# Causal attention and feed network: query tiles outermost, the feed's steps between the score blocks

## The reference

```
x = x + layernorm(attention(layernorm(x)))    # causal, low-rank terms added to every weight
h = layernorm(x)
for blk in range(3):
    h = h + linear2(gelu(layernorm(linear1(h)) * gamma + beta))    # 256 to 256, 4-bit weights scaled
x = x + layernorm(h)
```

## Time and profile before

| | us |
|---|---|
| median of 3 runs (1530.27 to 1532.49) | 1530.82 |
| the profiled execution, its own time | 1532.92 |
| its span in the trace | 1531.2 |
| of it: weights and projections, to the first score product | 177.3 |
| attention, to the last product with v | 1031.1 |
| feed | 322.8 |

### The profile page before, as it was taken

How to read it: one execution, slowest core, us unless ns; L and a number is a source line. 1 busy time by engine, 2 the same in 40 slices (tenths; PEclk the granted TensorE clock), 3 DMA queues, 4 the chain that set the end, 5 groups by cost and what they waited for, 6 DMA issues and landing times. The chain is left out here.

```text
span 1531.2 us, 27338 instructions
## 1 busy us (share of the span) xinstructions
PE 1415.8 (92%) x8838; PEld 621.7 (41%) x8838; DVE 319.3 (21%) x871; ACT 1218.0 (80%) x1552; POOL 315.9 (21%) x938
## 2 busy tenths in 40 slices
PE   6899499999989999998999998999999879997995
PEld 2455222222322223232223232222232558886784
DVE  3366100000000000000000000000000285578756
ACT  1366399999979999997999998999999555545644
POOL 0121100000120000021000012000010166446754
PEclk7699699999989999998999999999999999998998
DMA  5165751001130110022001012100000310011001
GB/s 142 60 227 190 140 128 28 29 29 28 49 93 1 28 28 29 29 71 71 24 6 29 29 45 79 45 2 1 1 1 8 129 58 1 1 56 55 1 1 55
DMA packets 60327, 77.62 MB, mean 51 GB/s; under 512 B 16016, under 2 KB 31376, under 8 KB 60176
## 3 DMA queue, kind: packets, MB, share of 16 engines
q1 hardware_dynamic: 52704, 68.79, 15.4%
q10 hardware_dynamic: 7472, 6.92, 1.8%
HBM read 50.50 MB, written 25.17 MB: 49 GB/s over the span
## 5 line engine op out<-in xcount | busy, mean ns | idle before, releaser
L729 ACT ACTIVATE probs<-S 128x1024 f32<-128x1024 f32 (+3 forms) x1152 | 981.3, 1173 | 70.8 <-PE S L761 67.0
L779 PE MATMUL O<-probs,vg 128*32 128x512 f32 (+3 forms) x4608 | 578.8, 575 | 0.6 <-POOL probs L702 0.5
L761 PE MATMUL S<-q_op,k_op 64*128 64x512 f32 (+3 forms) x2304 | 502.4, 480 | 44.4 <-DMA k_op<-qk_rows 17.4
L761 PEld LDWEIGHTS S<-q_op,k_op 64*128 64x128 f32 x2304 | 213.7, 187 | 604.8 <-ACT probs L729 562.3
L702 POOL TENSOR_SCALAR_AFFINE_SELECT probs<-probs 128x256 f32<-128x256 f32 x256 | 102.7, 406 | 928.1 <-ACT probs L729 919.7
L929 PE MATMUL psC<-wfT,yTC 128*128 128x256 f32 x768 | 175.1, 386 | 7.9 <-ACT yTC L990 5.5
L741 DVE COPY acc<-O 128x512 f32 x16 | 11.1, 691 | 777.1 <-PE O L779 777.1
L929 PEld LDWEIGHTS psC<-wfT,yTC 128*128 128x128 f32 x768 | 146.6, 194 | 29.5 <-ACT yTC L990 7.1
L779 PEld LDWEIGHTS O<-probs,vg 128*32 128x32 f32 x4608 | 91.5, 108 | 138.6 <-issue 118.3
L977 ACT ACTIVATE yC<-uC,nmrC,rstdC 128x256 f32<-128x256 f32 x128 | 66.3, 590 | 56.4 <-POOL nmrC L93 56.3
L984 ACT COPY yTC<-psC 128x1024 f32<-128x1024 f32 x32 | 31.6, 1007 | 56.0 <-PE psC L922 56.0
(11 more groups left out here) (96 smaller groups left out, 729.7 us busy)
## 6 DMA issues: line engine op xcount, KB each, us to landing
qk_rows<-parts SPq DMA_DIRECT2D x32, 512.0 KB, 3.1
q_op<-qk_rows SPq DMA_DIRECT2D x256, 64.0 KB, 2.3
k_op<-qk_rows SPq DMA_DIRECT2D x240, 64.0 KB, 2.3
acc_sums<-acc SPq DMA_DIRECT2D x16, 256.0 KB, 2.1
xC<-in_L_attn_x SPq DMA_DIRECT2D x8, 512.0 KB, 4.8
acc<-acc_sums SPq DMA_DIRECT2D x4, 1024.0 KB, 6.3
out<-uC SPq DMA_DIRECT2D x8, 512.0 KB, 3.1
acc<-in_L_attn_x ACTq DMA_DIRECT2D x6, 512.0 KB, 4.7
```

The costliest lines, as they stand in the source:

```text
L729: nc.scalar.activation(probs[:, pair % NP, :, 0:TT - q0], S[:, pair % NS, :, 0:TT - q0], ACT.Exp, scale=SCALE).then_inc(exp_ok, 1)
L761: last = nc.tensor.matmul(S[:, pair % NS, a, 0:TT - q0], k_op[mine, pair % 2, kb * P:(kb + 1) * P], q_op[mine, pair % 2, j * TT + q0:(j + ...
L779: last = nc.tensor.matmul(O[h * STRIP:(h + 1) * STRIP, o % 2, q0:TT], vg[:, kb, h, :], probs[:, (2 * b + h // 2) % NP, h % 2, 0:TT - q0], ...
```

## The change

The stages `attend` and `feed` become one, `attend_and_feed`, and the loops of the attention are turned inside out. Query tiles come first, in rising order, then the 4 groups, which makes 32 visits (`VISITS`); a visit goes through the key blocks of its tile from the diagonal down. As soon as a tile's four visits are done its feed can begin, in two halves of 256 tokens. A planner, `plan()`, places the 22 PE steps of a tile's feed between the blocks of later visits: from block 26 on, one tile per 76 blocks, and onto the end of a visit where one is within 1.7 blocks. Of the 154 steps of tiles 0 to 6, 27 stand at the end of a visit. The last tile's 22 steps follow the last block. It also fixes the order of the work on DVE, ACT, POOL and SP by a simulated run with costs that are written into it (full exponential 0.14 + 0.735, product 1.8, turn 0.6, layernorm 3.3, gelu 3.6, eight-DMA load 3.6).

`q_op` and `k_op` are now rings: 3 slots of a tile for q, 8 slots for k, so that each of the 144 chunks of keys (one tile of keys for one visit) is loaded anew. `O` has one buffer, and one PSUM bank `F` serves the feed. DVE turns `O` in 32 by 32 squares (`turn_o`), divides, turns back, and SP moves the result with 4 DMAs to `attT`. Layernorm including the inverse square root is on DVE alone. The gelu stands among the exponentials on ACT. V is kept as 17 columns per head for all heads, so the copies from `v_all` to `vg` on POOL go away. PE waits once per block for both pairs.

```diff
-                    for pair in (2 * b, 2 * b + 1):
-
-                        pe.wait_ge(exp_ok, i * NPAIR + pair + 1)
...
+                    if first and v:
+                        pe.wait_ge(o_out, v)
...
+                def score(b):
+                    v, t, c, kb, q0 = BLOCKS[b]
+                    if b == 0 or BLOCKS[b - 1][0] != v:
+                        pe.wait_ge(q_in[v % QS], LOAD * (v // QS + 1))
+                    if kb % NB == 0:
+                        pe.wait_ge(k_in[c % RING], LOAD * (c // RING + 1))
+                    if 2 * b + 1 >= NS:
+                        pe.wait_ge(exp_ok, 2 * b + 2 - NS)
+                    for n in (2 * b, 2 * b + 1):
+                        for a in range(2):
...
+    steps = {}
+    boundary = [LAST[v] + LAG for v in LAST]
+    for t in range(NT - 1):
+        for n, (name, k) in enumerate((name, k) for name in STEPS for k in range(2)):
+            at = FEED_FROM + FEED_EACH * (t + n / (2 * len(STEPS)))
+            near = min(boundary, key=lambda b: abs(b - at))
+            at = near if abs(near - at) < 1.7 else int(at)
+            steps.setdefault(at, []).append((name, t, k))
+    pe = []
+    for b in range(NBLK + LAG):
+        if b < NBLK:
+            pe.append(("score", b))
+        if b >= LAG:
+            pe.append(("weigh", b - LAG))
+        pe += steps.get(b, [])
+    pe += [(name, NT - 1, k) for name in STEPS for k in range(2)]
...
+                    else:
+                        m, t = int(x[0][-1]), x[1]
+                        for k in range(2):
+                            act.wait_ge(dve_ok[k], done[f"copy{m}", t, k])
+                        for c in range(NC):
+                            col = m * NC + c
+                            last = nc.scalar.activation(zT[:, c, :], zT[:, c, :], ACT.Gelu, bias=g["beta"][:, col:col + 1],
+                                                        scale=g["gamma"][:, col:col + 1])
+                        last.then_inc(gelu_ok, 1)
...
+                    if x[0] == "turn_o":
+                        v = x[1]
+                        dve.wait_ge(pv_ok, LAST[v] + 1)
+                        if v:
+                            dve.wait_ge(o_ready, v)
+                        nc.vector.transpose(o_turned[:, :, :].rearrange("p b e -> p (b e)"), O[:, :]).then_inc(o_out, 1)
+                        continue
...
+                for x in order["SP"]:
+                    if x[0] == "k_load":
+                        c = x[1]
+                        v, s = CHUNKS[c]
+                        if c >= RING:
+                            sp.wait_ge(scored, 2 * CHUNK_END[c - RING] + 2)
+                        with sp.Fori(0, 1):
+                            load_rows(sp, d, k_op[:, c % RING, :, :], 1, VISITS[v][1], slice(s * TT, (s + 1) * TT), k_in[c % RING], LOW + need)
...
+                    for b in range(NB):
+                        last_v = nc.vector.tensor_tensor(v_heads[:, bass.ds(n * NB + b, 1), :, 0:D].rearrange("p o h e -> p (o h) e"),
+                                                         psV[:, b, :].rearrange("p (h e) -> p h e", e=D),
+                                                         g["bv"][:, :].rearrange("p (h e) -> p h e", e=D), ALU.add)
```

More of the change, by code:

```diff
@@ L612, in _ @@
                         pe.sem_inc(op_used, 1)
-def attend(nc, g, d):
+HT = TT // 2
+HB = HT // P
+LAG = 2
+NS, NP = 3, 6
+RING, QS, AS = 8, 3, 3
+VISITS = [(t, i) for t in range(NT) for i in range(NG)]
+CHUNKS = [(v, s) for v, (t, i) in enumerate(VISITS) for s in range(t, -1, -1)]
+BLOCKS = [(v, t, c, s * NB + b, b * P if s == t else 0)
+          for c, (v, s) in enumerate(CHUNKS) for t in (VISITS[v][0],) for b in range(NB)]
+NBLK = len(BLOCKS)
+LAST = {v: n for n, (v, _, _, _, _) in enumerate(BLOCKS)}
@@ new lines, with feed_parts @@
+CHUNK_END = {c: n for n, (_, _, c, _, _) in enumerate(BLOCKS)}
+DIAG = [n for n, (_, t, _, kb, _) in enumerate(BLOCKS) if kb >= t * NB]
+STEPS = ["project", "turn_x"] + [f"{x}{m}" for m in range(BLK) for x in ("first", "turn", "second")]
+FEED_FROM, FEED_EACH = 26.0, 76.0
+def feed_parts():
+    parts = [("x_load", "SP", 1.0, ()), ("project", "PE", 1.8, ("moved",)), ("evac_att", "DVE", 0.75, ("project",)),
+             ("ln_att", "DVE", 3.3, ("evac_att",)), ("add_x", "DVE", 1.2, ("ln_att", "x_load")), ("ln_x", "DVE", 3.3, ("add_x",)),
+             ("norm_x", "DVE", 0.5, ("ln_x",)), ("turn_x", "PE", 0.6, ("norm_x",)), ("copy_x", "DVE", 0.75, ("turn_x",))]
+    h_at = "copy_x"
+    for m in range(BLK):
+        out = f"add{m}" if m < BLK - 1 else "evac_h"
+        parts += [(f"first{m}", "PE", 1.8, (h_at,)), (f"evac{m}", "DVE", 0.75, (f"first{m}",)), (f"ln{m}", "DVE", 3.3, (f"evac{m}",)),
+                  (f"norm{m}", "DVE", 0.5, (f"ln{m}",)), (f"turn{m}", "PE", 0.6, (f"norm{m}",)),
+                  (f"copy{m}", "DVE", 0.75, (f"turn{m}",)), (f"second{m}", "PE", 1.8, (f"gelu{m}",)),
+                  (out, "DVE", 0.8, (f"second{m}",))]
+        h_at = out
+    return parts + [("ln_h", "DVE", 3.3, ("evac_h",)), ("result", "DVE", 1.1, ("ln_h",)), ("store", "SP", 0.5, ("result",))]
@@ new lines, in attend_and_feed @@
+def attend_and_feed(nc, g, d):
+    order, _ = plan()
+    done = {}
+    for e in ("PE", "DVE"):
+        total = [0, 0]
+        for x in order[e]:
+            if len(x) == 3:
+                total[x[2]] += 1
+                done[x] = total[x[2]]
+    steps = [x for x in order["PE"] if len(x) == 3]
+    place = {x: n for n, x in enumerate(steps)}
+    gelus = {x: n + 1 for n, x in enumerate(x for x in order["ACT"] if x[0] != "exp")}
+    cuts = {n: m + 1 for m, n in enumerate(x[1] for x in order["POOL"])}
@@ L631, in attend @@
[L631 to L655, removed]
+        two = lambda n, s: [sb(f"{n}{k}", s)[(slice(None),) * len(s)] for k in range(2)]
+        vg = g["vg"]
+        k_op = sb("k_op", [P, RING, PAIRS, TT], F32R)
```

697 lines of the change are left out of this document (326 added, 371 removed).

## The result

| | before | after |
|---|---|---|
| median of 4 runs each on one chip, us | 1531.65 (1530.27 to 1533.18) | 1677.82 (1675.55 to 1678.74) |
| ratio, 95% interval | | 1.0952 (1.0933 to 1.0971) |
| span of the profiled execution | 1531.2 | 1675.7 |

The change makes the kernel 9.5% slower. The forecast was 1496 us, range 1445 to 1562, with 0.27 on slower. It had the wrong sign, and the time lies outside the range.

What follows compares the result with a forecast made beforehand. ACT paced the old attention; PE was to become the bound between the blocks. Block 48 at 272, plus 1097 to 1369, 33 for the last full blocks to 1402, tail 92: 1494, with 1.7 outside 1496 us, range 1445 to 1562.

Steps and rivals of the forecast that it cites:

- rival 2: Visit ends: the turn of O waits behind DVE's layernorm or a later step, 2.6 us more each, +62, 1558; chance 14%.
- Rival 3: Full blocks: four score products take PE itself 0.83 us, not 0.66, so no room exists, +70, 1566; chance 6%.
- rival 4: Better hiding: visit ends filled fully, half the stalls gone, the clock holds in the tail, 1448; chance 20%.
- rival 1: Longer table switches: each gelu stops ACT for 2.4 us more than taken, +50, 1546; chance 8%.
- the stall of a gelu: Between the blocks: PE stalls 2.6 us at each of 21 gelus while ACT is away, 55 us.
- the single wait: PE's one wait per block for both pairs was taken to be worth 0 by itself.
- The feed's steps: Feed products and turns between blocks 48 and 557: 198 us of PE work, plus 15 for weight loads laid bare.
- The start: Up to block 48, paced by SP's loads, then the second tile's last visit and three feed steps: block 48 at 272.
- The tail: Last tile's bare feed after the last block, thrice 16.7 us in it: 92 us, 5 for the clock, bounds 83 and 105.
- The middle: Block 48 to the last product with v, 1130 us: PE work 1018, gelu stalls 55, visit ends 24, last full blocks 33.
- the visits' ends: PE waits at each visit's end for DVE's turn of the single O: 1.0 us net per end, 24 us.
- room in the full blocks: PE needs 1.66 us of a full block's 1.833, so 0.17 us to spare per block for feed steps.

Runs made afterwards that it cites:

- e4: The kernel after without the feed of tiles 0 to 6 (attention and the last tile's feed stay): 1348.40 us, ratio 0.8804 to the kernel before.
- e2: The kernel after with each feed product of tiles 0 to 6 cut into two halves one block apart: 1690.48 us, ratio 1.1038.
- e11: e10 with the feed's steps placed from block 30 on, 77 blocks per tile, instead of 26 and 76: 1533.10 us, ratio 1.0002.
- e5: The kernel before with a single wait per block for both pairs and nothing else: 1535.56 us, ratio 1.0021.
- e3: The kernel after with PE again waiting for each pair's slot alone: 1647.77 us, ratio 1.0759.
- e1: The kernel after with the feed's gelu replaced by an exponential, so the table loads go and the feed's values change: 1583.75 us, ratio 1.0341.
- e9: The kernel after with the first three loads of queries issued by ACT instead of SP: 1670.45 us, ratio 1.0901.
- e12: e10 with the feed's steps placed from block 34 on, 75 blocks per tile: 1542.90 us, ratio 1.0065.
- e8: The kernel after with the second half of the last tile's feed steps writing to a free score bank: 1669.20 us, ratio 1.0893.
- e10: The kernel after with the edits of e3, e7, e8 and e9 together, the last tile keeping the gelu: 1540.49 us, ratio 1.0065.
- e7: The kernel after with the gelu computed from a polynomial on DVE and a tanh on ACT: 1591.07 us, ratio 1.0383.

## Why the forecast was wrong

**Right.** The front (0), the first score product (180.18 for 180.3), the skeleton's attention (e4: from block 48 on 941 us, where 949 go by the old pace), the length of a gelu on ACT (4.13 for 4.3; the 0.3 for lost overlap isn't there), key loads hidden after tile 2 (PE has no wait for one there), and PE as the bound between the blocks (e2, e11). Its 7.5 us from step to step takes every step for a product; by its own 29.5 us per tile it is 7.1, still above ACT's 6.3. DVE is 36% busy in the middle (457.7 of 1269), less than the 45% given, and PE's waits for the turn of `O` come to some 7 us in the whole run, so rival 2 is out. The two rows count the same waits, once for the load of the weights and once for the products behind it:

```profile
PEld O L929 <- DVE o_turned L1028: 6.7, 4, 5.6
PE O L929 <- DVE o_turned L1028: 5.8, 2, 5.4
```

Rival 3 fell with e5, rival 4 with the result itself, and rival 1 had the right place with the wrong price: the switch is no longer than I took, what it does to PE is.

**The step that failed: the stall of a gelu, "(4.3 + 0.97 - 2.65) = 2.6 x 21 = 55".** It is mis-sized in each of its last two terms (0.97 stands there for the 0.92 of the sentence before it, which makes 1 us and isn't what failed). For 2.65 us of work left to PE the timeline shows one block, 1.86 from 887.40 to its end at 889.26. For one exponential to be waited for, it shows two, 1.99: that is the single wait, and e3 has one. 4.13 + 1.99 - 1.86 gives the stop of 4.26. Even the gelu without table loads stops PE, for 1.45 us on average in e1, where my formula gave nothing; 21 of those are 30 us. And the clock behind the stop was no term at all, though the earlier trace rows had shown me 0.68 on a PE that is idle for most of a stretch; I had put it into the tail alone. The table loads' part of this, stop and clock, is 94 us by e1. With the 30 that stay in e1 the gelus cost some 124 us where the forecast had 55.

**"The single wait by itself is worth 0."** It costs some 3 us in the kernel before and 30 in the new one. The argument ("where PE bounds, neither wait holds") looked at blocks in steady stream only, and left out the block behind each feed step.

**The feed's steps.** I took 1.83 us for a product with its exposed load and 0.54 for a turn. The timeline of the kernel after has:

```profile
858.03 1.99 PE L969 MATMUL F<-zT,wfT 128*128 128x256 f32 x8
859.96 0.73 PE L913 MATMUL S<-q_op,k_op 64*128 64x512 f32 x4
...
879.54 0.66 PE L960 MATMUL F<-ident,yC 128*128 128x128 f32 x4
880.13 0.73 PE L913 MATMUL S<-q_op,k_op 64*128 64x512 f32 x4
```

That is 1.93 and 0.59 from start to start: 98 x 0.10 + 56 x 0.05 = 13 us. That is too little to change the sign.

**The start, +25.7.** In e4, without the feed, block 48 starts at 285.3. The forecast without its 2.7 us for feed steps is 269.3, so 16 us are lost without any feed: a load takes SP 3.8 to 4.0 us, as reckoned, but a move 2.4 instead of 1.9, and the visits wait for queries that stand behind moves. By e9 SP's queue has a part in it; how the 16 divide no run shows. The first feed steps take 12.4 us (297.7 - 285.3) where I had 2.7, another 9.7. The timelines of SP and PE in the kernel after:

```profile
272.66 2.43 SPq L857 DMA_DIRECT2D attT<-o_div  x4
275.20 3.88 SPq L489 DMA_DIRECT2D q_op<-qk_rows  x8
```

```profile
264.36 1.09 PE L960 MATMUL F<-ident,yC 128*128 128x128 f32 x4 [7.92 <-DVE yC L1018]
```

PE reached the turn 7.9 us before its layernorm was done, DVE being in the layernorms of both halves. That is close to the wait that I had named as the one that would make the forecast wrong, though PE waits here for what the turn reads and not for the bank. It isn't the main cause: e12 has it with 8.1 us and e11 with 3.7.

**The tail, +29.8.** The first part came out: 6.3 us to the first product, as predicted, and 18.8 from there to the first turn for 19.8. In the whole tail six products take 3.4 to 3.8 us instead of 1.99 and five turns 1.09 instead of 0.63, 12.5 us where I had 5 for the clock; the bank costs 8.6 by e8. What is left, 29.8 - 7.5 - 8.6 or about 14 us, no run took apart. The place is known: the forecast has "thrice 16.7", and from the first product of a block to the next block's it is 30.3 us (1585.5 to 1615.8) and 24.1 (to 1639.9). In the first of them DVE takes 13.1 us from the first evacuation to the last copy, where I had 9.5.

**The middle, +126.** The tanh and the wait per pair take 120 us out of it (1256 to 1136 in e10), where the forecast had 55 for all stalls of gelus. The other 61, which e10 still has over the forecast without those 55, are what follows.

**Why there was no gain even without the stops.** e11's middle takes 1134 us, close to the 1130 of the forecast by chance, since those contained 55 of gelu stalls. Without them the forecast is 1075. Of the 59 us between, 13 are the dearer steps. The other 46, with the 24 reckoned for the visits' ends, make 70 us; the window of e11 has PE idle for 1134.0 - 1085.8 = 48 of them, and its clock of 0.98 makes some 20 more as an estimate (2% of 1086). What PE waited for in e11's middle can be read off (columns as in the earlier trace rows):

```profile
PE F L980 <- DVE yC L1044: 23.8, 8, 6.4
PE S L931 <- ACT probs L904: 18.0, 24, 1.8
```

Half of the 48 are eight waits of the feed's turns for their layernorm on DVE, the longest 6.4 us; 18 are waits for exponentials. The forecast had nothing for the first kind in the middle. Whether another order on DVE would avoid them stays open.

The balance against the kernel before can be written out with e11. The start takes 25 us more than at the old pace (284 for 259). The middle at the old pace would be 949, so it takes 185 more: 213 + 13 of feed steps, less 72 of room in the full blocks (414 x 0.173) and 40 on the diagonals (24 x 1.66), plus the 70. The tail is 113. That is 25 + 185 + 113 = 323 us for the feed, and the stage that was dissolved took 322.8. This must come out so, since e11 takes as long as the kernel before and the 70 were found as the rest; it sorts the costs and proves none. The room of 72 and 40 us is the forecast's, which no run measures by itself. Measured are the start, the tail, PE's 48 idle us and its clock, and they, with the dearer steps, are what eats the gain. The table loads, the single wait, the tail's one bank and the queue of SP then put the 137 us on top by which the kernel after is slower than e10.

## What to carry to other kernels

If the engine that feeds TensorE's loop uses one table set, keep every other function in that set or out of the loop: here 21 gelus of 1.5 us cost 94 us more by their table loads, some two fifths of it TensorE's clock around the stop. Price such an interruption by what the waiting engine has left to do in its slots, what it must wait for on return, and what its clock does then. Two waits merged into one cost next to nothing (3 us) only while the waiting engine is never late; and a small surplus per block fills up only with work that is there at that block, so it can't pay for a step many times its size.

## What the runs showed of the hardware

The granted clock falls with a single stop. In a stop of 4.26 us it goes from 1.00 to 0.50 and stays there till 897.9, so that a block takes 3.01 us instead of 1.66; it does so at all 21 gelus, and a window of 200 us has 0.93. After 1.41 us a block takes its 1.66 still, and the window's clock is 1.00. That holds for 17 of e1's 21 stops; at four the clock was lower in the 3 us that follow, and e1's middle as a whole has 0.98. A table load takes 1.28 us here and starts at most 0.02 us behind the instruction before it, there and back. Exponential and tanh alternate without any (e7: one load in the whole run).
